# Counting edges through five small slots, and a neighbour sum from split operands, in a graph-network kernel on one core

## The reference

```python
deg = segment_sum(ones(E), dst, n)
inv_deg = where(deg > 0, 1 / maximum(deg, 1), 0)
def sage_conv(h, W_l, b_l, W_r):
    aggr = segment_sum(h[src], dst, n) * inv_deg
    return aggr @ W_l + b_l + h @ W_r
# four experts of two layers each, relu after each layer; the top two of four softmax gates weigh them
```

## Time and profile before

| | us |
|---|---|
| median of three runs | 2082.97 |
| lowest, highest | 2076.41, 2086.34 |
| the profiled execution, its own time | 2078.46 |
| its span, first to last instruction | 2076.6 |
| PE busy | 1867.6 (90%) |
| DVE busy | 893.1 (43%) |
| ACT, POOL busy | 632.9, 581.7 |

### The profile page before, as it was taken

One profiled execution on the slowest core, in us unless ns is written; L12 is line 12 of the kernel. 1 busy time (PEld: TensorE's weight loads), 2 busy tenths in 40 slices (PEclk: granted clock), 3 DMA queues, 4 the chain that ended last, 5 costly groups with the idle time before them and its releaser, 6 DMA issues. The chain is left out here.

```text
span 2076.6 us, 26808 instructions
## 1 busy us (share of the span) xinstructions
PE 1867.6 (90%) x9514; PEld 1507.0 (73%) x9515; DVE 893.1 (43%) x1804; ACT 632.9 (30%) x1170; POOL 581.7 (28%) x502
## 2 busy tenths in 40 slices
PE   2777897999999999996999988999998998899994
PEld 1344456888888878884779887788777898778883
DVE  8877721111111113654656545522275654562236
ACT  7722112111112121101554652222256365232210
POOL 0000214231414133311622102544454121064422
PEclk9999999999999999998999999999999999999997
DMA  2010502131412046723560200111137211011012
GB/s 59 1 50 0 161 0 87 56 131 40 146 40 106 36 172 230 196 96 107 144 199 26 91 21 0 41 41 41 59 79 190 99 54 59 1 41 41 23 53 65
DMA packets 76957, 160.11 MB, mean 77 GB/s; under 512 B 10128, under 2 KB 25162, under 8 KB 75218
## 3 DMA queue, kind: packets, MB, share of 16 engines
q1 hardware_dynamic: 76858, 158.80, 24.3%
HBM read 103.24 MB, written 55.53 MB: 76 GB/s over the span
## 5 line engine op out<-in xcount | busy, mean ns | idle before, releaser
L578 PE MATMUL ps<-yT,wslot 128*128 128x500 f32 (+1 forms) x576 | 207.3, 360 | 8.2 <-ACT qpT L1603 4.9
L580 PE MATMUL ps<-yT,wslot 128*128 128x500 f32 (+1 forms) x576 | 205.8, 357 | 0.0
L579 PE MATMUL ps<-yT,wslot 128*128 128x500 f32 (+1 forms) x576 | 205.7, 357 | 0.0
L828 PE MATMUL ps<-g,adj 125*128 125x512 f32 (+1 forms) x800 | 187.9, 397 | 3.5 <-issue 3.5
L828 PEld LDWEIGHTS ps<-g,adj 125*128 125x128 f32 (+1 forms) x800 | 151.3, 189 | 40.0 <-issue 3.9
L1954 POOL TENSOR_TENSOR wslot<-mix_landing,wslot 128x512 fp32r<-128x512 f32 x96 | 127.0, 1353 | 181.8 <-ACT wslot L1540 181.8
L1959 POOL TENSOR_TENSOR hidT<-qpT,hidT 128x500 fp32r<-128x500 f32 (+1 forms) x96 | 103.2, 1079 | 213.7 <-DVE hidT L1744 213.7
L1603 ACT ACTIVATE qpT<-ps,all_cols 128x500 f32<-128x500 f32 (+1 forms) x96 | 58.1, 610 | 313.7 <-PE ps L580 267.7
L362 PE MATMUL ps<-key_hot,row_hot 125*125 125x500 bf16 x430 | 105.6, 385 | 46.6 <-DVE key_hot L333 36.1
L578 PE MATMUL ps<-parts,w 128*128 128x500 f32 (+1 forms) x384 | 136.3, 355 | 6.1 <-DVE bl L947 6.1
L579 PE MATMUL ps<-parts,w 128*128 128x500 f32 (+1 forms) x384 | 136.1, 354 | 0.0
(11 more groups left out here) (275 smaller groups left out, 3635.3 us busy)
## 6 DMA issues: line engine op xcount, KB each, us to landing
mix_landing<-in_L_mix_W SPq DMA_DIRECT2D x16, 1024.0 KB, 5.1
qk_dram<-qk_parts SPq DMA_DIRECT2D x128, 125.0 KB, 2.4
g_dram<-staged SPq DMA_DIRECT2D x40, 256.0 KB, 2.0
u_dram<-staged SPq DMA_DIRECT2D x40, 256.0 KB, 2.0
g_in<-g_dram SPq DMA_DIRECT2D x40, 256.0 KB, 3.6
u_in<-u_dram SPq DMA_DIRECT2D x40, 256.0 KB, 2.7
k_stack<-qk_dram SPq DMA_DIRECT2D x8, 1250.0 KB
q_stack<-qk_dram SPq DMA_DIRECT2D x8, 1250.0 KB
```

The costliest lines, as they stand in the source:

```text
L578: nc.tensor.matmul(out, lhs_high, rhs_high, start=first, stop=False)
L579: nc.tensor.matmul(out, lhs_high, rhs_low, start=False, stop=False)
L580: return nc.tensor.matmul(out, lhs_low, rhs_high, start=False, stop=last)
L828: last = nc.tensor.matmul(m.ps[0:counts.shape[1], t % 2, :], counts if exact else counts.bitcast(F32), part if exact else part.bitcast(F32 ...
```

## The change

- The counting ring has five slots of two chunks instead of two halves of five. A round still has ten chunks.
- The loop over turns is written out for 25 groups. DVE and PE read the table for group g + 1 before they work on group g, and PE opens the bank of group g + 1 before it counts group g.
- ACT writes the counts into a ring of two buffers `kept`. SP moves each group from there in two DMAs: one to `adjT` in SBUF (now laid out by group), one to `adj_dram`, in 1250 pieces of 50 counts (200 bytes). ACT's copy also sums each row of the group (`group_sums`). SP waits for all of them before the block ends. The ten stores of the next block are gone.
- Gate weights, gate bias and the experts' bias block are loaded in the counting block.
- The first sum takes `xn` in high and low float32r halves, two products for each source tile, times the counts; the moving operand is now ten (or five) pieces of 50. ACT and POOL make the halves, two feature blocks before the sums and two beside them.
- The degrees come from thirty PE products of ones with `adjT` in float32r. The DVE reduction and the column form are gone; `inv_col` comes from ten turns. The inversion goes by chunk, between the first `mean` steps.
- A bound on the counts (POOL's reduction across partitions of `group_sums`) is loaded to a register by PE after the gates; one branch picks float32 or float32r for degrees and sums together. The experts' branch is lifted out of its loop.
- The first two weight blocks are loaded at once and split in this block (ACT, DVE), in a place that the turned `xn` frees, and the bias block is turned here.

The diff, cut to its core:

```diff
-HALF = 5
-ROUND_CHUNKS = 2 * HALF
+SLOTS, SLOT_CHUNKS = 5, 2
+ROUND_CHUNKS = SLOTS * SLOT_CHUNKS
...
+                def move_counts(g):
+                    sp.wait_ge(banks_free, BANKS + g + 1)
+                    sp.dma_start(m.adjT[:, g].bitcast(F32), kept[:, g % KEPT_RING]).then_inc(kept_moved[g % KEPT_RING], 16)
+                    sp.dma_start(adj_dram[g // BANKS, 0:P, :, g % BANKS * DG:(g % BANKS + 1) * DG], kept[:, g % KEPT_RING])\
+                        .then_inc(kept_moved[g % KEPT_RING], 16)
...
+                for n in range(KEPT_RING):
+                    sp.wait_ge(kept_moved[n], 32 * len(range(n, NG, KEPT_RING)))
...
                 def keep_counts(turn, bank):
...
+                    if g >= KEPT_RING:
+                        act.wait_ge(kept_moved[g % KEPT_RING], 32 * (g // KEPT_RING))
+                    nc.scalar.activation(kept[:, g % KEPT_RING], m.ps[0:P, bank, 0:GW].rearrange("p (d s) -> p s d", s=T),
+                                         ACT.Copy, accum_out=m.group_sums[:, g:g + 1]).then_inc(banks_free, 1)
...
+                        for s in range(SLOTS):
+                            vec.wait_ge(slots_free, (before + j) * SLOTS + s + 1)
+                            for b in range(SLOT_CHUNKS):
+                                last = nc.vector.tensor_scalar(key_hot[:, s, b, :], m.hot[0:CE, :],
+                                                               group_key[:, bank, bass.ds(at + s * SLOT_CHUNKS + b, 1)], None, ALU.is_equal)
...
-                with pe.Fori(1, GROUP_TURNS) as turn:
-                    for bank in range(BANKS):
-                        count_group(turn, bank)
+                for g in range(BANKS, NG):
+                    if g + 1 < NG:
+                        following = decode(pe, g + 1)
+                        open_bank(g + 1)
+                    count_group(g, entry)
+                    entry = following
...
-                for n in range(PIECES):
-                    for p0, p1 in ((0, EVEN), (EVEN, P)):
-                        sp.dma_start(adj_dram[n, p0:p1], m.adjT[p0:p1, n]).then_inc(adj_stored, 16)
...
+                    for i, (d0, dn) in enumerate(CHUNKS):
+                        for s in range(T):
+                            last = nc.tensor.matmul(m.ps[:, i, 0:dn].rearrange("p (g d) -> p g d", d=DG), operand(m.ones_r[0:P, :]),
+                                                    operand(m.adjT[:, d0 // DG:(d0 + dn) // DG, s, :]), start=(s == 0), stop=(s == T - 1))
...
                         for s in range(T):
-                            last = nc.tensor.matmul(m.ps[:, 4 + n % RING, 0:cn].rearrange("p (q d) -> p q d", d=SPAN),
-                                                    m.xn[:, s, f * 128:(f + 1) * 128], m.adjT[:, c0 // SPAN:(c0 + cn) // SPAN, s, :], start=(s == 0), stop=(s == T - 1))
+                            for h in range(2):
+                                part = half(h == 0, f, s)
+                                last = nc.tensor.matmul(m.ps[:, 4 + n % RING, 0:cn].rearrange("p (g d) -> p g d", d=DG),
+                                                        operand(part), operand(m.adjT[:, c0 // DG:(c0 + cn) // DG, s, :]),
+                                                        start=(s == 0 and h == 0), stop=(s == T - 1 and h == 1))
...
+                pe.wait_ge(small_ready, TOP_READY)
+                top_sum = pe.value_load(m.top_sum[0:1, 0:1], min_val=0, max_val=E)
+                with pe.If(top_sum > EXACT_COUNTS):
+                    sums(False)
+                with pe.Else():
+                    sums(True)
...
+                act.wait_ge(xn_low, K)
+                for n in range(2):
+                    act.wait_ge(m.landed[n], 16)
+                    nc.scalar.activation(m.w1[:, n, 0], m.landing[:, n], ACT.Copy).then_inc(m.w_high, 1)
...
+                    mean_of(i)
+                weight_low(0)
+                mean_of(NC3)
+                weight_low(1)
```

More of the change, by code:

```diff
@@ L213, in _ @@
                 act.wait_ge(consts_made, 8)
+                nc.scalar.activation(m.ones_r[:], m.ones[:], ACT.Copy)
                 act.wait_ge(edges_copied, 1)
@@ L323, in _, with key_hots @@
                 vec.drain()
-                def key_hots(turn, bank):
-                    lo, rounds, before = decode(vec, turn * BANKS + bank)
+                def key_hots(g, entry):
+                    lo, rounds, before = entry
+                    bank = g % BANKS
                     with vec.Fori(0, rounds) as j:
                         at = first_chunk(lo, j)
[L329 to L334, removed]
-                            last.then_inc(hots_ready, 1)
-                for bank in range(BANKS):
-                    key_hots(0, bank)
+                        vec.wait_ge(keys_ready, g + 1)
+                        for s in range(SLOTS):
[3 more added lines that the diff above has]
+                                                               group_key[:, bank, bass.ds(at + s * SLOT_CHUNKS + b, 1)], None, ALU.is_equal)
+                            last.then_inc(hots_ready, 1)
+                entry = decode(vec, 0)
+                for g in range(BANKS):
+                    following = decode(vec, g + 1)
+                    key_hots(g, entry)
+                    entry = following
                 for h in range(2):
@@ L344, in _, with open_bank, count_group @@
                                             ALU.subtract, ALU.mult).then_inc(xn_ready, 1)
-                with vec.Fori(1, GROUP_TURNS) as turn:
-                    for bank in range(BANKS):
-                        key_hots(turn, bank)
+                for g in range(BANKS, NG):
+                    following = decode(vec, g + 1) if g + 1 < NG else None
+                    key_hots(g, entry)
+                    entry = following
             @block.tensor
             def _(pe):
[L351 to L355, removed]
+                def open_bank(g):
+                    pe.wait_ge(banks_free, g + 1)
+                    nc.tensor.matmul(m.ps[0:P, g % BANKS, 0:GW], zeros[:, 0:P], zeros[:], start=True, stop=False)
+                def count_group(g, entry):
+                    acc = m.ps[0:P, g % BANKS, 0:GW]
+                    lo, rounds, before = entry
                     with pe.Fori(0, rounds) as j:
@@ L375, in _ @@
                 pe.wait_ge(ranges_ready, 1)
-                for bank in range(BANKS):
-                    count_group(0, bank)
+                entry = decode(pe, 0)
+                open_bank(0)
+                for g in range(BANKS):
+                    following = decode(pe, g + 1)
+                    open_bank(g + 1)
+                    count_group(g, entry)
+                    entry = following
                 for t in range(T):
@@ L465, in _ @@
[L465 to L474 removed]
+                            last.then_inc(small_summed, 1)
```

302 lines of the change are left out of this document (169 added, 133 removed).

## The result

| | before | after |
|---|---|---|
| median, 20 runs each | 2080.75 us (2074.05 to 2086.34) | 2087.07 us (2080.64 to 2095.35) |
| ratio after / before | | 1.0031 [1.002, 1.0043] |
| profiled execution, own time | 2078.46 | 2088.53 |
| last product of the counting (closing) | 208.48 | 225.82 |
| first gate product | 212.73 | 265.31 |

By the bound of 0.5% this is no change, near its slow edge. The table holds the whole story: at the first gate product the changed kernel is 52.6 us behind, at the experts' first product 10.0. So the part from the first gate product on saved 42.6 us (33.6 + 7.9 = 41.5 were forecast) and something ahead of the gates took it all.

What follows compares the result with a forecast made beforehand. Before the sums PE and DVE wait for each other; in the first sum PE is the bound. 10.0 - 1.9 + 33.6 + 7.9 = 49.6 us off 2078.5 gives 2028.9, forecast as a 2031 us median, range 2014 to 2048.

Steps and rivals of the forecast that it cites:

- Counting ring: Counting: five small slots shorten rounds in long groups and steps between groups; 10 us saved, bounds 0 to 16.
- Rival (2): Counting keeps its time because both engines' issue, not the ring, sets the round; 2041 us, chance 0.13.
- Counts out by transfers: Moves out of the two buffers: nothing lost within counting, gates wait for the last move; 1.9 us lost.
- nothing within counting: Moves during counting: a buffer turn of 5.9 us for two groups stays under PE's pace, so no loss there.
- (4): Ring of two buffers becomes the clock of counting, seen in ACT's wait ahead of its copy; 2108 us, chance 0.03.
- (1): Store of 200-byte pieces costs twice the 640-byte one, landing 7.2 us; 2042 us, chance 0.13.
- (3): Sums and degrees: products with pieces of 50 run no faster than plain ones, 0.427 us; 2075 us, chance 0.04.
- First sum: From the end of the gates to the last sum: float32r products take 58.0 us instead of 91.6; 33.6 us saved.
- handover: Between last sum and experts' first product: weight splits move ahead of the means, leaving 2.9 us; 7.9 us saved.
- The register load and the branch: On PE after the gates: idle 3.5 us plus 1.0 us for the lowered clock.
- POOL's new work: Before POOL's four low halves: some 6 us of new work, all beside gates and degrees.

Runs made afterwards that it cites:

- e12: Changed kernel with both moves cut at partition 112 and the store written in pieces of 2000 bytes (values change, timing only): 2026.66 us, ratio 0.9739.
- e7: Kernel without moves (e3), PE's turn of the inverted degrees two sums later, DVE's copy of it behind the gates: 2021.3 us, ratio 0.9712.
- e3: Changed kernel without buffers and moves: ACT copies straight into adjT in its former layout, stores of five groups go out cut: 2029.3 us, ratio 0.9737.
- e4: Kernel without moves (e3) with the old counting ring of two slots of five chunks: 2028.72 us, ratio 0.9749.
- e11: Kernel without moves and with the late turn (e7), with the old counting ring of two halves of five chunks: 2029.09 us, ratio 0.9754.
- e5: Changed kernel with only the store into adj_dram cut at partition 112: 2044.41 us, ratio 0.981.
- e6: Changed kernel with only the move into adjT cut at partition 112: 2058.48 us, ratio 0.9887.
- e1: Changed kernel with both moves of each group cut at partition 112, pieces still 200 bytes: 2036.86 us, ratio 0.9776.
- e9: Kernel before the change with its five adjacency stores uncut, rows of 10000 bytes: ratio 0.9992.
- e10: Kernel before the change with its five adjacency stores cut at partition 120 instead of 112: ratio 0.9997.
- e8: Kernel without moves (e3) with POOL's four low halves put behind DVE's small subtraction: 2024.4 us, ratio 0.9733.
- e2: Changed kernel with the store uncut but in 125 pieces of 2000 bytes (values change, timing only): 2047.51 us, ratio 0.9839.

## Why the prediction was wrong, point by point

**Counting ring, 10.0 us.** Right in kind, 2 to 4 us too high. The rounds of a long group on PE and DVE, changed kernel:

```profile
55.22 2.33 PE L390 MATMUL ps<-key_hot,row_hot 125*125 125x500 bf16 x10 [0.64 <-ACT row_hot L244]
56.17 2.68 DVE L355 TENSOR_SCALAR key_hot<-hot,group_key 125x500 bf16<-125x500 f16 x10 [0.29 <-PE ps L390]
58.19 2.33 PE L390 MATMUL ps<-key_hot,row_hot 125*125 125x500 bf16 x10 [0.64 <-DVE key_hot L355]
59.14 2.69 DVE L355 TENSOR_SCALAR key_hot<-hot,group_key 125x500 bf16<-125x500 f16 x10 [0.28 <-PE ps L390]
61.16 2.33 PE L390 MATMUL ps<-key_hot,row_hot 125*125 125x500 bf16 x10 [0.64 <-DVE key_hot L355]
62.49 2.68 DVE L355 TENSOR_SCALAR key_hot<-hot,group_key 125x500 bf16<-125x500 f16 x10 [0.67 <-PE ps L390]
```

Inside a group 2.97 us apart (2.87 forecast, 3.14 before), so the added waits cost 0.1 us of the 0.27; the step is 3.35 (3.37 forecast). One-round groups are 3.67 us apart in e12 (3.63 before), no gain, as forecast. Where no move holds counting, the last count stands at 200.8 (e12) to 202.5 (e7) instead of 208.5: 6.0 to 7.7 us. Of these the small slots are 5.3 (e3 and e4) or 5.4 (e7 and e11). With the old ring and the groups written out it stands at 207.4 (e4) and 207.9 (e11), so the writing out gives 1 us or less. Rival (2) falls with the same runs.

**Counts out by transfers, 1.9 us lost: this is the step that failed.** Forecast: gates at 204.6; they start at 265.31, 60.7 us later. The profiled execution came out at 2088.5 instead of 2028.9, 59.6 later. So this one term holds the whole miss, but for the 2 to 4 us that the ring fell short. The working took the `out` store as the nearest row, "a store that also has 1250 pieces, of 640 bytes", and put its 3.6 us of landing on each move. Three things were wrong in that. First, the row says x2: this store is cut at partition 112, and the diff's new transfers are not. I compared pieces and bytes and never the partition ranges. Second, I let the two transfers of a group overlap at no price (one landing of 3.6 us for both), while they share a queue; e5 and e6 show both to count. Third, I took a turn as one latency of 5.9 us for two groups. What the runs showed in its place is a queue that is never empty: 6.6 us for each group's two transfers at 75 GB/s, hence a turn of 13.7 us, over PE's pace of 3.6 to 3.7 a group. The bounds, half to twice the landing, came from the same row, so they could not hold 9.4 us. That "nothing within counting" is lost rested on the same 5.9.

The Trainium skill has the rule that speaks here (DMA: Bandwidth & Descriptors, Why a DMA increments its semaphore by 16 and not by 1): the number of engines is the largest up to 16 that divides the outer dimension of both sides. For 125 this gives 5, for 120 it gives 15. The runs agree: shares of 0.31 and 0.90 to 0.96, the last a little above 15/16. I had drawn on the same page for its 512-byte rule alone.

**The rivals.** (4) was the mechanism: ACT's wait ahead of its copy, with a turn of 13.7 us. I gave it 0.03 and asked for "a store three times as slow as its neighbour", which is what 5 engines of 16 are. It asked for a turn over 14.5 us, and with 13.7 the kernel was indeed not slower by more than the bound. Its price was right: worked by its own sum at the turn and landing measured (13.2 to 13.7 and 9.4 us), counting takes 132 to 137 us instead of 88 and the end 5.8 more, 2081 to 2086 in all, and 2087 was measured. What was wrong was the chance that I gave it. (1) was half true: its cause is real, but alone, beside a cut, it costs 4 us up to the gates and some 10 in the median. (3) falls: the products of the sums come 0.235 us apart, not 0.427.

**First sum, 33.6 us, and handover, 7.9 us.** Right in the total, in part by luck. Sums forecast 46.2 us, measured 49.0 (284.2 to 333.2, of which 1.3 are the turn of the inverted degrees): a product of ten pieces of 50 comes every 0.235 us instead of 0.229, and those of five pieces every 0.12 us, so the pieces cost 2 to 3% and no more. Degrees forecast 5.8, measured 6.2 (6.02 in pieces of 250, e3). The register load and the branch were put at 4.5 us with the clock; the timeline of the changed kernel has PE go from the bias turn to the degrees without a gap, so 4.5 us too many there offset 3.2 too few in the sums and degrees:

```profile
265.31 11.48 PE L507 MATMUL ps<-xnT,gw 128*4 128x500 f32 x24 [39.33 <-PEq L171]
276.73 0.23 PE L509 MATMUL ps<-ident,bl_rows 16*128 16x16 f32 x1
276.88 6.20 PE L518 MATMUL ps<-adjT,ones_r 125*128 125x500 f32 x30
283.02 1.25 PE L523 MATMUL ps<-ident,inv_row 4*125 4x4 f32 x10
```

The gate products themselves take 1.2 us more than before (11.48 instead of 10.25); the granted clock of the 13 us ahead of them is 0.50. The experts' first product comes 2.2 us after the last sum (2.9 forecast).

**What I held hidden and was not:** POOL's new work "beside gates and degrees". It is beside PE, but it can hold DVE. In the changed kernel this does not show (0.45 us). With the moves mended or gone, PE waits for DVE 6.8 us (e1), 7.0 (e5) and 5.0 (e3) in the profiled executions with a long hold, with a clock of 0.67 behind it in e3, and not at all in those with a short one. From the first gate product to the experts' first it is 78.6 us in e1 and 69.0 in e12.

## What to carry to other kernels

When a diff adds a transfer, compare its partition range, not only its bytes and pieces, with its nearest row: a DMA share that stays at 0.3 to 0.4 while everything waits for DMA is the sign that most engines may not be in use, and here a cut into 112 and 13 partitions mended it. When transfers follow each other without a gap, price them by their rate against the pace of the engines, and not by one landing. Ask of each new transfer whether a small ring waits for it, for the same missing cut cost nothing in a store that nobody waited for. And when a large forecast gain does not show, add up the marks of the stages first: here they told that 42.6 us had come and 52.6 had gone.

## What the runs showed of the hardware that I had not expected

- **Five engines of 16.** A transfer over 125 partitions keeps the share at 0.31 and moves 132 GB/s (e9). Cut at 112 it moved 310 and 272 GB/s in the two windows of 6 us, cut at 120 it moved 318 and 380 (before, e10). With pieces of 200 bytes the uncut store moves 53 GB/s (changed kernel).
- **POOL holds a DVE instruction with two inputs in SBUF.** The 40-element subtraction took 0.20 us with POOL idle (e8). Beside POOL it took 0.34 (e11), 0.45 (changed kernel), 1.67 (e7), 1.75 (e12), 1.79 (e6), 1.85 (e2), 2.02 (e4), 7.15 (e3), 9.40 (e1) and 9.67 (e5). It always ended within 0.1 us of the end of one of POOL's instructions (2.84 us each). In e1, e3 and e5 it did not go ahead at the first such end but only behind the last of the four; in the others it went at the next one. What decides this no run here settles. The profiled executions of e1, e3 and e5 are each the slowest of their runs (so is e6's, with a short hold); whether the others were spared it, no trace shows, so the medians of these three hold an unknown share of it. DVE's reciprocals, with one input, took 3.28 us beside POOL (e7) as without it (e3). The Trainium skill (SBUF — State Buffer, SBUF: two separate sides) describes an exclusive lock on a port pair that the two engines share, held for one whole instruction. The traces agree that DVE is held; that it can be held over several of POOL's instructions goes beyond what the section says.
- **A branch can be free.** The same register load and branch cost PE nothing in the changed kernel, 1.0 to 1.2 us in e11, e3 and e7, 2.0 in e4, and 3.5 in the earlier trace rows. Why, no run here settles.
